# Conv block with lambda layer on one Trainium2 core: the four stores and the four loads of v are issued by ScalarE instead of SyncE

## The reference

```
n   = groupnorm(x)                                  # 32 groups over 512 channels
h   = relu(bn1(conv1x1(n, w1)))                     # 512 -> 128 channels
q   = bnq(conv1x1(h, wq))                           # 128 -> 64  (4 heads x 16)
k   = softmax over 16 channels of conv1x1(h, wk)
v   = bnv(conv1x1(h, wv))                           # 128 -> 32
pos = 15 x 15 convolution of each channel of v with 16 filters (emb)
out = q . (k v^T) + q . pos                         # content and position, 4 heads x 32
y   = bn3(conv1x1(relu(bn2(out)), w3))              # 128 -> 512
return x + relu(y + n)
```

## Time and profile before

| | before |
|---|---|
| median of 3 runs | 5176.27 us |
| profiled execution, its time | 5191.58 us |
| profiled execution, span of the instructions | 5188.9 us |
| TensorE matmul busy | 4668.3 us, 90% |
| VectorE busy | 2959.6 us, 57% |
| ScalarE busy | 2285.5 us, 44% |
| GpSimd busy | 748.1 us, 14% |
| queue of SyncE's DMAs (q1) | 1017.22 MB, 60.1% of 16 engines' span |
| queue of ScalarE's DMAs (q10) | 260.05 MB, 13.5% |

### The profile page before, as it was taken

One profiled execution on the slowest core, in us unless ns is written; L12 is line 12 of the kernel. 1 busy time (PEld: TensorE's weight loads), 2 busy tenths in 40 slices (PEclk: granted clock), 3 DMA queues, 4 the chain that ended last, 5 costly groups with the idle time before them and its releaser, 6 DMA issues.

```text
span 5188.9 us, 120753 instructions
## 1 busy us (share of the span) xinstructions
PE 4668.3 (90%) x49366; PEld 2754.3 (53%) x49366; DVE 2959.6 (57%) x4695; ACT 2285.5 (44%) x2816; POOL 748.1 (14%) x433
## 2 busy tenths in 40 slices
PE   4989999998999999999989998999988999999997
PEld 2555555554555555555545555555555555555554
DVE  4456555565555565655655555655556565566564
ACT  1444445444444444444444444444444444444443
POOL 0011110111111111101111111111011111111111
PEclk8899999899999989999899989899999999998998
DMA  3678767778777787677787777876777867778776
GB/s 96 224 241 292 261 215 257 245 259 292 231 236 253 252 281 266 217 249 248 257 290 234 232 256 246 287 261 210 256 249 260 289 226 236 248 253 290 254 221 227
DMA packets 537170, 1284.13 MB, mean 247 GB/s; under 512 B 43048, under 2 KB 225324, under 8 KB 528556
## 3 DMA queue, kind: packets, MB, share of 16 engines
q1 hardware_dynamic: 471276, 1017.22, 60.1%
q10 hardware_dynamic: 65472, 260.05, 13.5%
HBM read 844.79 MB, written 432.33 MB: 246 GB/s over the span
## 4 chain that ended last, share of the span: by engine, by line
PE 63%; issue 11%; DVE 9%; DMA 5%; SPq 4%; ACT 4%; POOL 3%; ACTq 0%; DVEq 0%; POOLq 0%
PE ring L522 16%; PE ring L503 14%; PE ring L648 13%; PE ring L578 7%; PE ring L602 4%; DMA X<-x_dram 3%; PE ring L529 3%; POOL X L1171 2%; PE ring L534 2%; PE ring L612 2%; SPq L358 2%; DVE S L1015 2%; ACT region L696 1%; DVE region L696 1%; DMA q_parts<-region 1%
## 5 line engine op out<-in xcount | busy, mean ns | idle before, releaser
L696 ACT COPY region<-ring 126x1024 f32<-126x1024 f32 x1184 | 1163.9, 1016 | 1157.0 <-PE ring L503 1147.8
L578 PE MATMUL ring<-h,w3T 128*128 128x512 f32 x2048 | 1015.6, 639 | 108.4 <-DVE S L1015 76.7
L503 PE MATMUL ring<-Qt,Ep 96*126 96x256 bf16 x5120 | 855.7, 309 | 112.5 <-ACT region L696 62.8
L522 PE MATMUL ring<-X,w1e 128*128 128x512 f32 x2048 | 907.8, 596 | 28.8 <-DVE w1e L892 28.8
L648 PE MATMUL ring<-region,V 126*32 126x128 f32 x24576 | 879.9, 288 | 24.9 <-issue 24.7
L503 PEld LDWEIGHTS ring<-Qt,Ep 96*126 96x126 bf16 x5120 | 628.9, 153 | 358.8 <-issue 181.8
L648 PEld LDWEIGHTS ring<-region,V 126*32 126x32 f32 x24576 | 678.6, 115 | 246.9 <-issue 236.1
L696 DVE COPY region<-ring 126x1024 f32<-126x1024 f32 x352 | 430.3, 1222 | 646.7 <-PE ring L503 646.7
L868 DVE BATCH_NORM_STATS2 st<-X 128x6 f32<-128x512 f32 x1024 | 624.7, 680 | 199.2 <-DMA X<-x_dram 199.1
L578 PEld LDWEIGHTS ring<-h,w3T 128*128 128x128 f32 x2048 | 388.5, 201 | 536.1 <-issue 387.6
L522 PEld LDWEIGHTS ring<-X,w1e 128*128 128x128 f32 x2048 | 385.0, 191 | 496.3 <-issue 493.0
(11 more groups left out here) (127 smaller groups left out, 2980.1 us busy)
## 6 DMA issues: line engine op xcount, KB each, us to landing
X<-x_dram SPq DMA_DIRECT2D x132, 2048.0 KB, 21.0
out_dram<-X SPq DMA_DIRECT2D x512, 512.0 KB, 9.8
X<-x_dram ACTq DMA_DIRECT2D x124, 2048.0 KB, 9.8
Qt<-q_parts SPq DMA_DIRECT2D x768, 128.0 KB, 3.0
V<-v_windows SPq DMA_DIRECT2D x96, 1024.0 KB, 8.1
lambda_sums<-S SPq DMA_DIRECT2D x64, 1024.0 KB, 3.9
h<-lambda_sums SPq DMA_DIRECT2D x256, 256.0 KB, 5.2
q_parts<-region SPq DMA_DIRECT2D x128, 256.0 KB, 4.1
```

The costliest lines, as they stand in the source:

```text
L503: last = nc.tensor.matmul(dst[0:TROWS, i * 256:(i + 1) * 256], taps(u, xo, yo), Q[:, :, xo * BLK + yo, :], start=(i % 2 == 0), stop=True, ...
L522: last = nc.tensor.matmul(dst[:, hh * HALF:(hh + 1) * HALF], w1e[:, c, :], X[:, j, c, hh * HALF:(hh + 1) * HALF], start=(c == 0), stop=(c ...
L578: last = nc.tensor.matmul(dst[:, yb * HALF:(yb + 1) * HALF], w3T[:, t, :], src, start=True, stop=True)
L696: return engine_copy(dst, src)
```

## The change

`store_v` and `load_v` are moved, word for word, from SyncE's program to ScalarE's. ScalarE issues the four stores in `front` at `k3`, between `spread_v` and `softmax_exp`; it issues the four loads in the prologue ahead of `w0.0`, and in the loop at the name `o1.2`. Semaphores, sizes and addresses are the same.

```diff
@@ SyncE
-            def store_v(im):
-                sp.wait_ge(vpad_ready, im * 3 + 3)
-                sp.wait_ge(vx_ready, im * (3 * NCH) + 3 * NCH)
-                for a, n in ((0, 8), (8, 8), (16, 5)):
-                    sp.dma_start(vD[PAD:PAD + W, a:a + n, :],
-                                 vX[:, 0:n, a // BLK:a // BLK + NYB, :].rearrange("x r m v -> x r (m v)"))\
-                        .then_inc(v_out, 16)
-                sp.dma_start(vR[PAD:PAD + W, :], vX[:, 5, 2:2 + NYB, :].rearrange("x m v -> x (m v)"))\
-                    .then_inc(v_out, 16)
-            def load_v(im):
-                sp.wait_ge(v_out, im * 64 + 64)
-                for t in range(3):
-                    ...
-                    sp.dma_start(V[:, t, :, :], src).then_inc(v_in[t], 16)
-                sp.dma_start(Vrem, ...).then_inc(vrem_in, 16)
@@ SyncE, prologue
                 load_q(0, j)
-            store_v(0)
-            load_v(0)
@@ SyncE, loop
                 store_q(b + 1, 3)
-                store_v(b + 1)
                 load_q(b + 1, 3)
-                load_v(b + 1)
@@ ScalarE: the same two functions with act in place of sp
@@ ScalarE, front
                     spread_v(im, j)
+                    if j == NCH - 1:
+                        store_v(im)
                     softmax_exp(im, j)
@@ ScalarE, prologue
             for name in PRO:
+                if name == "w0.0":
+                    load_v(0)
@@ ScalarE, loop over MIX
                     for n in late:
                         relu_half(b, n)
                     late = []
+                    if name == "o1.2":
+                        load_v(b + 1)
```

More of the change, by code:

```diff
@@ L359, in load_q @@
                         .then_inc(q_in[j], 16)
-            def store_v(im):
-                sp.wait_ge(vpad_ready, im * 3 + 3)
-                sp.wait_ge(vx_ready, im * (3 * NCH) + 3 * NCH)
-                for a, n in ((0, 8), (8, 8), (16, 5)):
-                    sp.dma_start(vD[PAD:PAD + W, a:a + n, :],
-                                 vX[:, 0:n, a // BLK:a // BLK + NYB, :].rearrange("x r m v -> x r (m v)"))\
-                        .then_inc(v_out, 16)
-                sp.dma_start(vR[PAD:PAD + W, :], vX[:, 5, 2:2 + NYB, :].rearrange("x m v -> x (m v)"))\
-                    .then_inc(v_out, 16)
-            def load_v(im):
-                sp.wait_ge(v_out, im * 64 + 64)
-                for t in range(3):
-                    src = bass.AP(vD.tensor, t * TROWS * ROW, [[ROW, P], [BLK * WROWS * ROW, NXB], [1, ROW]])
-                    sp.dma_start(V[:, t, :, :], src).then_inc(v_in[t], 16)
-                sp.dma_start(Vrem, bass.AP(vR.tensor, 0, [[ROW, WCOLS], [BLK * ROW, NXB], [1, ROW]])).then_inc(vrem_in, 16)
             def load_v3(b):
@@ L715, in bn2_relu, with store_v, load_v @@
                 nc.scalar.activation(part, part, ACT.Relu, bias=pbi[:, 1:2], scale=psc[:, 1:2]).then_inc(h2_ready, 1)
+            def store_v(im):
+                act.wait_ge(vpad_ready, im * 3 + 3)
+                act.wait_ge(vx_ready, im * (3 * NCH) + 3 * NCH)
+                for a, n in ((0, 8), (8, 8), (16, 5)):
+                    act.dma_start(vD[PAD:PAD + W, a:a + n, :],
+                                 vX[:, 0:n, a // BLK:a // BLK + NYB, :].rearrange("x r m v -> x r (m v)"))\
+                        .then_inc(v_out, 16)
+                act.dma_start(vR[PAD:PAD + W, :], vX[:, 5, 2:2 + NYB, :].rearrange("x m v -> x (m v)"))\
+                    .then_inc(v_out, 16)
+            def load_v(im):
+                act.wait_ge(v_out, im * 64 + 64)
+                for t in range(3):
+                    src = bass.AP(vD.tensor, t * TROWS * ROW, [[ROW, P], [BLK * WROWS * ROW, NXB], [1, ROW]])
+                    act.dma_start(V[:, t, :, :], src).then_inc(v_in[t], 16)
+                act.dma_start(Vrem, bass.AP(vR.tensor, 0, [[ROW, WCOLS], [BLK * ROW, NXB], [1, ROW]])).then_inc(vrem_in, 16)
             def softmax_exp(im, j):
```

## The result

The change makes the kernel slower: 5423.62 us (median of four runs, 5411.85 to 5437.93) against 5175.89 us, a ratio of 1.0482 with a 95% interval of 1.0456 to 1.0509. Forecast were 5340 us and a range of 5245 to 5420. So the direction was right, and the loss of 248 us was half again as large as the 164 us forecast; the time lies just outside the range.

A forecast was written before the change was run, and what follows sets the result against it. VectorE was taken as the bound from `k3` to `o3.0`, TensorE elsewhere. 5191.58 + 165.5 + 12 - 10.4 - 3 = 5355.7 us profiled; with the profiled execution 15.3 us above the median, 5340 us, range 5245 to 5420.

The forecast's parts named there:

- The bound, and where a delay counts: From `k3` to `o3.0` VectorE is the bound; whatever delays it there delays the round, in all 31 rounds.
- Issue times of the stores on ScalarE: Four stores ahead of the exponential hold ScalarE 6.3 us; less 1.1 slack, VectorE moves 5.34 us a round, 165.5 us.
- The clock term: TensorE at half speed in `cl` after the longer idle stretch, sometimes into `o2.0`: 0.4 us a round, 12 us, ends 0 and 46.
- the same terms of the sum: VectorE's delay 165.5 us, half-speed clock 12, less 10.4 of q waits and 3 from earlier output stores and x loads.
- The loads on ScalarE cost, I say, nothing: Four loads at `o1.2` hold ScalarE 5.5 us; VectorE's wait for GpSimd at `o2.3` has 4.5 us of cover: no cost.
- The gain at q: With v's stores off SyncE, `load_q(3)` moves up; TensorE's wait for q outside the prologue vanishes, at most 10.4 us saved.
- rival 1: V's loads on another queue collide with q's, delaying `w0.0`: 71 to 93 us more, 5410 to 5435 us; chance 0.12.
- Rivals 2 to 4: Chances 0.06, 0.05, 0.15: short store issues, 5180 us; SyncE's relief decides, 5148 us; hold 3 to 5 us, 5250 us.
- Rival 3: SyncE's relief decides: VectorE's stretch not lengthened; q, output and x come sooner; 28.7 us off, 5148 us; chance 0.05.

The follow-up runs named there:

- The pauses: Kernel before, no DMA moved, with 23, 25 or 27 chained tiny ScalarE copies ahead of each image's last exponential: 5246.79, 5288.68 and 5352.89 us.
- stores alone: Kernel before with only the four stores of v moved to ScalarE, ahead of the exponential; loads stay on SyncE behind `load_q(3)`: 5324.60 us, ratio 1.0314.
- a pause: Only v's stores on ScalarE, loads on SyncE, plus 32 chained tiny ScalarE copies at `o1.2` where the change issues the loads: 5446.10 us, ratio 1.0522.
- run 78: Not a run number: 78 us is the added time of the kernel before with 23 tiny ScalarE copies ahead of each image's last exponential, 5246.79 us.

## Why the prediction was wrong in size

- **The bound, and where a delay counts: right.** From `k3` to `o3.0` VectorE sets the pace.
- **Issue times of the stores on ScalarE: right.** 5.7 us for the four in the round shown, 6.3 forecast; the reading that the third and fourth store of the series are long whoever issues them held (3.23 us for three, 2.48 for the fourth). The wait ahead of `cl` is 5.3 us at the median, 5.8 forecast, and the stage ahead of it is 4.9 us longer, 5.34 forecast.
- **The clock term: half speed behind the idle stretch right, the size and the place wrong.** I put 0.4 us a round at `o2.0`, and called less than nothing impossible. The pauses show that 4.2 us more of wait ahead of `cl` make a round only 2.5 us longer (78 / 31), and 5.0 us more make it 5.8 us longer (181 / 31), with most of the difference in `lam`. (The half speed in the earlier trace rows lasted 3.4 us and not 3.6.) For stores alone the errors cancel: 156 us measured, where the same terms of the sum (165.5 + 12 - 10.4 - 3) make 164.
- **"The loads on ScalarE cost, I say, nothing": this is the step that failed**, by 99 us. It asked only whether VectorE waits for GpSimd at `o2.3`. Three points were missed. GpSimd's addition moves onto VectorE's small operations of `cp`, 11 times, 2.0 us each, 22 us; a pause shows this effect without any DMA. The hold was 7.7 us at the median of all rounds and not 5.5 (6.4 at least, 11.5 at most). And q lands late, 36 us. These two are 58 of the 99 us; VectorE waits 7 us for GpSimd at the output tiles, and the rest isn't taken apart.
The Trainium skill, "SBUF — State Buffer", section "Who interferes with whom", says that VectorE and GpSimd share one pair of SBUF ports, that VectorE needs it only in some cases (a copy or cast in one of its two-port modes, or an operation with two inputs in SBUF), and that whoever comes first then has it for the whole instruction while the other is fully blocked. The trace agrees: L1002 took 2.30 us in place of 0.18 and ended with GpSimd's L1173, and L1015, with one input in PSUM, was never held up.
- **The gain at q: wrong in sign for the change.** 10.4 us were to be saved; TensorE waits 48.3 - 12.4 = 35.9 us outside the prologue. With the stores alone on ScalarE the gain was there (no wait outside the prologue): the loads of V reverse it. This is rival 1, given 0.12, and the measured 5424 us lies in its 5410 to 5435. That is luck in part: only 36 of its 71 to 93 us are there. Its 10.0 us of landing came from the earlier trace rows, where it belongs to q's second quarter (the last quarter's longest was 4.4), and with V's loads beside them the last quarter's loads took 6.3 to 6.9 us. It looked at the loads of q and not at the store, which loses as much. Its weight was set too low because I counted slack after the 5.3 us delay: with the delay taken away, the same traffic costs 137 us of waiting. The two costs hide each other, so they don't add: moving the stores back cures one and lays the other bare.
The Trainium skill, "DMA: Bandwidth & Descriptors", section "Queues, rings and completion order", has a DMA engine take turns between the queues that have work for it. The trace agrees: the last quarter of q takes 6.3 to 6.9 us to land with V's loads on a second queue, 2.7 before.
- **Rivals 2 to 4: out.** The hold was neither under 2 us nor 3 to 5 us, and TensorE's clock in the first half of `lam` was 0.82, no higher than before (0.84). Rival 3's gain from a relieved SyncE exists, where neither hold nor traffic stands against it, and is 0.2 to 0.3% instead of 0.6%.

Not settled: why TensorE's time at half speed rises so steeply between 4.6 and 5.5 us of wait, and in a stage 30 us away. A kernel that keeps TensorE busy during the wait might have told; it wasn't tried.

TensorE's unexplained issue time in the small matmuls (L591), 106.3 us, has hardly grown. Before, it stood at two lines:

```profile
PE ring L612 <- issue: 68.8, 35, 2.4
PE ring L648 <- issue: 24.7, 14, 3.4
```

With the one or two at `w0.0` it is 51 stalls and 100.1 us before, 51 and 111.7 after. They look like waits for instructions. The profile has a DMA queue for these, with 16 KB a packet:

```profile
q8 instruction: 415, 6.80, 0.5%
```

In the traces of before and after each of the 51 stalls ends 2.3 to 3.2 us after one of these packets started, where a moment taken at random has one at that distance in 7% of cases. No run changes the loading of instructions, so the cause is read from this coincidence alone.

## What to carry to other kernels

Moving a DMA to another engine's queue moves three things: its issue time, into that engine's order, its bytes, out of the order of the queue, and every instruction behind it, onto other engines' work. Ask of each what it now meets; here the order on one queue had kept a bulk transfer behind the one that was needed first. And when one cost delays everything, the slack behind it isn't real: price the others as if it were gone.

## What the runs showed of the hardware

- Of the four stores of v issued in a row, the first two hold their engine for some 0.6 us each, the third for 2.0 and the fourth for 2.4 (medians on ScalarE's queue; 2.2 and 2.5 on SyncE's), in the prologue as in the loop. The four loads of V held ScalarE for 7.7 us in the change, 6.7 to 7.0 at the other places, and SyncE for 5.7 (medians).
- A VectorE cast of 96x32 that is 0.18 us long took 2.3 us when GpSimd's addition of 128x1024 had just begun; a multiplication of 128x128 took 1.66 us in place of 0.29. Operations of VectorE with one input in PSUM kept their time.
- The same loads of q (six of 128 KB) landed in 2.7 us (the first in 3.9) with V's loads behind them on the queue, and in 6.3 to 6.9 with V's loads on a second queue.
- TensorE stood still 51 times, for 0.4 to 5.4 us, and each time went on 2.3 to 3.2 us after an instruction load had started: 100 us of the run before the change and 112 after.
- TensorE idle for 4.6 us ahead of `cl` in each round made the run 78 us longer, idle for 5.5 us 181 us (5352.89 - 5171.91); the mean granted clock was 0.933 and 0.894.
